# One core, gated cross attention and gated feed forward: the order of every engine's work laid out anew

## The chip, the core and the metric

The kernel runs on one core of one Trainium2 chip. The time is the device time of one execution in microseconds (us). A profile of another execution shows what every engine did. Engine names are those of the profile: PE is TensorE (its weight loads are PEld), DVE is VectorE, ACT is ScalarE, POOL is GpSimd, SP is SyncE, which here only issues transfers.

## The reference

Four batches of 512 rows with 256 columns. A layer norm, attention of 8 heads with depth 32 over a context whose mask in effect leaves the last 128 keys, a gated sum, another layer norm, and a feed forward of width 768 with integer weights.

```python
def attention(memory, query, mask, b):          # memory 4x512x512, query 4x512x256
    Q = split_heads(query, 8) * 32 ** -0.5
    K, V = (split_heads(part, 8) for part in jnp.split(memory, 2, axis=2))
    logits = jnp.einsum('bhqd,bhkd->bhqk', Q, K) + b[0] + -1e30 * (1 - mask)
    return merge_heads(softmax(logits) @ V)
def ffn(x, w_gate, w_up, w_down):               # weights int / 127
    h = silu(x @ w_gate.T) * (x @ w_up.T)
    return h @ w_down.T
x = x + tanh(g_xattn) * attention(ctx, layernorm(x), mask, b)
x = x + tanh(g_ffn) * ffn(layernorm(x), w_gate, w_up, w_down)
```

## The kernel before

The 2048 rows are worked in eight halves r = 0 to 7 of 256 rows; batch b has the halves 2b and 2b + 1. Values that must be exact go through TensorE as a high and a low float16 part. Every engine has its own instruction queue and works it strictly in order. The order is written out by hand: the table ORDER (L163) has one string of step codes per engine, and each engine's run() walks its string. A code is two letters, the half or batch, and after a dot a part. Semaphores alone hold the engines together: a step that needs another's result waits for a count.

The codes that the text uses, with the line of what they issue:

- sa (L968 to L977 on DVE, L658 on POOL): statistics of the first norm; na (L992 or L669) the norm, ha (L745) its high and la (L688) its low part. sa2, sa4 and sa6 take two halves at once. sb, nb, hb, lb are the same for the second norm (nb is L681).
- du (L1002, DVE): doubles the parts of q; qs (L1262) then turns them on TensorE for the halves 0 and 1, and qn (L591) turns them by two transfers on SP for the halves 2 to 7.
- kp, kr (L1048, L1040, L693): key parts; ks (L1272, L1277): key stack turned on TensorE and copied out by DVE (L1081, L1085) or ACT (L772). fr (L1013 to L1017) and ft (L1284, L1022) make the fillers that all key stacks but batch 0's need. br, mc, mt, eb are small steps for the mask. ys (L1059) is the scale of y.
- rm (L1333, and L1343 in batch 0, then L1122 on DVE): row maxima, four for each half; mx (L1358, L810) turns them. sc (L1378, L1380, then the exponential L821 on ACT): four for each half. ws (L1399, L1404, then L832, L834 on ACT): the weighing of the values. at (L1450 on PE, L1153 and L1155 on DVE, L698 on POOL): two for each half, adds the attention to x.
- nn (L582, SP): turns the second norm's parts by one transfer for the halves 0 to 6; nt (L1469, L860) does it on TensorE and ACT for half 7. wc (L781, ACT) casts a weight, wn (L573, SP) turns it; wn1 and wn0 are for hi, wn2 for do.
- hi (L1503): one of six hidden steps of a half, eight matmuls; ACT takes tanh (L869), pr (L1166, L1177) on DVE makes the product, hs (L878 on ACT, L705 on POOL) its two parts; do (L1529) is one of six down steps, four matmuls. fi (L939, L950, then L562, L559) adds and stores. ck, fs and sq check the ranges.
- wu (L1241): three or four matmuls on constants, whose results nobody reads. Ahead of all steps TensorE does 14 of them (L1218).

Work banks of PSUM are given out round robin by place in TensorE's string: four banks for the steps before hi0.0, and two from there on, since the other two belong to the hidden steps. A step that fills a bank waits until the one that used it last was emptied. hidden step n waits for product n - 2 (L1490). All loads are issued by SP and ACT ahead of their strings. The flag that is asked near the end decides whether a second, wide program follows; it does not here.

## Time and profile before

| | |
|---|---|
| time, median of 3 runs (range) | 137.76 us (137.49 to 138.76) |
| the profiled execution's own time | 137.66 us |
| its span, from the first to the last instruction | 135.8 us |
| PE busy | 125.0 us, 92% |
| DVE busy | 104.6 us, 77% |
| POOL busy | 94.0 us, 69% |
| ACT busy | 91.5 us, 67% |
| mean granted TensorE clock | 0.994 |

Busy time of PE counts a matmul from its start to its modelled end, so matmuls that follow each other overlap (an end stands 0.16 us behind the next start), and the distance between starts tells what one costs. A number in brackets at a row's end is the idle time ahead of it and what ended it.

### The profile page before, as it was taken

To read this page: it belongs to the slowest core of one execution; us is meant where nothing else is said; L and a number is where in the kernel's file an instruction comes from. 1 tells how busy PE (TensorE), PEld (TensorE's weight loads), DVE (VectorE), ACT (ScalarE), POOL (GpSimd) and SP (SyncE) were. 2 spreads that over 40 slices of the span, in tenths; PEclk is the share of its full clock that TensorE was granted. 3 is DMA by queue.
4 is the path that set the end of the run, shared out by engine and by line. 5 is a ranking of instruction groups with operands and counts; after the bars stand their busy time and mean duration, and the time that the engine had idled before them with its cause. 6 is when DMAs were issued, how large, how long until landed. Compare 5 with 4: busy or idle time off the path is not lost.

```text
span 135.8 us, 3716 instructions
## 1 busy us (share of the span) xinstructions
PE 125.0 (92%) x1276; PEld 97.6 (72%) x1276; DVE 104.6 (77%) x296; ACT 91.5 (67%) x206; POOL 94.0 (69%) x146
## 2 busy tenths in 40 slices
...
GB/s 127 285 127 369 370 352 155 119 186 89 83 157 116 77 5 76 97 58 7 0 165 234 69 2 57 25 0 0 75 84 0 5 233 1 77 7 47 30 86 92
DMA packets 32050, 14.08 MB, mean 104 GB/s; under 512 B 25605, under 2 KB 31257, under 8 KB 32025
## 3 DMA queue, kind: packets, MB, share of 16 engines
...
q14 instruction: 14, 0.11, 0.3%
...
HBM read 5.52 MB, written 2.10 MB: 56 GB/s over the span
## 4 chain that ended last, share of the span: by engine, by line
PE 60%; DVE 16%; POOL 9%; DMA 4%; issue 4%; SPq 3%; ACT 2%; DVEq 0%; ACTq 0%; POOLq 0%
PE ps L1503 26%; PE ps L1529 11%; DMA gates<-in_L_xattn_b_dram 4%; PE ps L1399 4%; PE ps L1404 4%; PE ps L1378 4%; PE ps L1380 4%; DVE max_cols L1122 4%; PE ps L1450 3%; PE ps L1333 2%; DVE stats L968 2%; POOL x_sb L698 2%; POOL h L705 2%; DVE gated L1166 2%; POOL q_parts L688 2%
## 5 line engine op out<-in xcount | busy, mean ns | idle before, releaser
L1503 PE MATMUL ps<-n_t,w_gu_t 128*128 128x256 f16 x384 | 49.0, 273 | 0.9 <-DVE h L1177 0.7
L1503 PEld LDWEIGHTS ps<-n_t,w_gu_t 128*128 128x128 f16 x384 | 36.4, 98 | 7.1 <-DVE h L1177 2.1
L705 POOL TENSOR_TENSOR h<-h 128x256 f16<-128x256 f32 x48 | 31.5, 674 | 7.5 <-ACT h L878 7.5
L1166 DVE SCALAR_TENSOR_TENSOR gated<-tanh_h,ps 128x256 f32<-128x256 f32 x48 | 19.9, 415 | 12.3 <-ACT tanh_h L869 11.9
L869 ACT ACTIVATE tanh_h<-ps 128x256 f32<-128x256 f32 x48 | 18.3, 382 | 13.1 <-PE ps L1503 10.9
L1529 PE MATMUL ps<-w_d_t,h 128*128 128x256 f16 x192 | 25.7, 273 | 0.0
L821 ACT ACTIVATE probs<-ps,exp_bias 128x512 f32<-128x512 f32 x32 | 21.6, 686 | 4.3 <-PE ps L1380 4.1
L1122 DVE TENSOR_REDUCE max_cols<-ps 128x4 f16<-128x512 f32 x32 | 21.4, 684 | 2.9 <-PE ps L1333 2.6
L1177 DVE SCALAR_TENSOR_TENSOR h<-ps,gated 128x256 f32<-128x256 f32 x48 | 20.4, 425 | 2.4 <-POOL h L705 0.8
L878 ACT ACTIVATE h<-h 128x256 f16<-128x256 f32 x48 | 18.5, 412 | 4.6 <-DVE h L1177 4.3
L1529 PEld LDWEIGHTS ps<-w_d_t,h 128*128 128x128 f16 x192 | 18.4, 98 | 2.1
L698 POOL TENSOR_TENSOR x_sb<-x_sb,attn 128x256 f32<-128x256 f32 x16 | 11.6, 733 | 8.7 <-DVE attn L1155 8.5
L1378 PE MATMUL ps<-q_stacks,k_stacks 128*128 128x256 f16 x64 | 15.6, 273 | 0.4 <-ACT max_rows L810 0.3
L1380 PE MATMUL ps<-max_rows,kv_rest 128*128 128x256 f16 x64 | 15.5, 273 | 0.0
L968 DVE BATCH_NORM_STATS2 stats<-x_sb 128x6 f32<-128x256 f32 x32 | 11.6, 413 | 4.6 <-DMA x_sb<-in_x_dram 2.5
L658 POOL TENSOR_TENSOR rstd<-var_eps,neg_half 128x2 f32<-128x2 f32 (+1 forms) x13 | 10.5, 806 | 6.7 <-DVE var_eps L977 6.6
L688 POOL TENSOR_TENSOR norm<-norm 128x512 f16<-128x512 f32 x8 | 9.3, 1160 | 6.4 <-ACT norm L745 6.2
L688 POOL TENSOR_TENSOR q_parts<-norm,q_parts 128x512 f16<-128x512 f32 x8 | 9.4, 1180 | 5.8 <-ACT q_parts L745 5.8
L1333 PE MATMUL ps<-k_stacks,q_stacks 128*128 128x128 f16 x128 | 12.1, 219 | 0.0
L1333 PEld LDWEIGHTS ps<-k_stacks,q_stacks 128*128 128x128 f16 x128 | 9.1, 98 | 2.3 <-issue 0.6
L681 POOL TENSOR_SCALAR norm<-x_sb,neg_mean,rstd 128x256 f32<-128x256 f32 x16 | 9.1, 579 | 0.5
L832 ACT ACTIVATE o_sb<-ps 128x512 f32<-128x512 f32 x8 | 4.8, 596 | 6.3 <-PE ps L1404 6.2
...
## 6 DMA issues: line engine op xcount, KB each, us to landing
...
q_stacks<-q_parts SPq DMA_TRANSPOSE x12, 3.3
```

Of the source, the lines that this page charges most:

```text
L688: pool.tensor_tensor(low, full, high, ALU.subtract).then_inc(norm_low, 1)
L705: pool.tensor_tensor(h16[:, r % 2, m, 1, :], h32[:, n % NHB, :], h16[:, r % 2, m, 0, :], ALU.subtract).then_inc(h_low, 1)
L821: act.activation(probs[:, j % NPB, :], bank32(SCORES[j % 2]), ACT.Exp, bias=key_bias[:, n:n + 1] if is_wide else exp_bias[:, b:b + 1], sca ...
L878: act.activation(h16[:, r % 2, m, 0, :], h32[:, n % NHB, :], ACT.Copy).then_inc(h_high, 1)
L1122: dve.tensor_reduce(dst, bank32(plan.bank(step)).rearrange("p (h k) -> p h k", h=HG), AX.X, ALU.max, negate=not is_wide).then_inc(emptied_ ...
L1166: mine(dve.scalar_tensor_tensor(out=gated[:, n % 2, :], in0=tanh_h[:, n % 2, :], scalar=1.0, in1=got[:, 0:SH], op0=ALU.add, op1=ALU.mult))
L1177: dve.scalar_tensor_tensor(out=dst, in0=got[:, SH:2 * SH], scalar=0.5 * W_SCALE * W_SCALE * H_SHRINK, in1=gated[:, n % 2, :], op0=ALU.mult ...
L1333: ins = pe.matmul(bank32(n)[:, j * P:(j + 1) * P], q_stacks[:, b, qt, h, :], k_stacks[:, b, h, :], start=(j == 0), stop=(b >= FILL_FROM an ...
L1378: pe.matmul(dst, k_stacks[:, b, h, :], q_stacks[:, b, 2 * half:2 * half + 2, h, :], start=(i == 0), stop=False, skip_group_check=True)
L1380: ins = pe.matmul(dst, (max_sel if is_wide else max_sel16)[:, h, :], (max_rows if is_wide else max_rows16)[:, rows, :], start=False, stop= ...
L1503: ins = pe.matmul(dst, lhs, rhs, start=(w == 0 and (k, l) == terms[0]), stop=(k, l) == terms[-1], skip_group_check=True)
L1529: ins = pe.matmul(dst, lhs, rhs, start=(m == 0 and l == 0 and (t == 0 or r == R - 1)), stop=(m == MT - 1), skip_group_check=True)
```

## The change: the five strings of the order

Only the strings of ORDER are other. Each engine has the same set of steps as before. The number of printed rows differs because equal neighbours are merged. The first line of PE's string, before and after, stands for the table:

```diff
     "pe": """
-        ks0 mt qs0.0 wu5 wu0 qs0.1 rm0.0 rm0.1 wu7 rm0.2 qs1.0 rm0.3 mx0 rm1.0 qs1.1 rm1.1 wu3 sc0.0 sc0.1 rm1.2 sc0.2
+        wu7 mt wu2 wu0 wu4 ks0 wu3 qs0.0 ft wu6 qs0.1 rm0.0 rm0.1 qs1.0 rm0.2 qs1.1 rm0.3 rm1.0 rm1.1 mx0 rm1.2 wu5
```

DVE at the program's start, from the first statistics of half 0 (`stats<-x_sb`). Before:

```order
L968 BN_STATS stats<-x_sb 128x6 x2
L972 BN_AGGR mv<-stats 128x2 x2
L977 TENSOR_REDUCE var_eps<-mv 128x2
L1048 TENSOR_SCALAR k_parts<-kv 128x8x64
L1007 TENSOR_SCALAR bias_row<-mask_row 1x128
L992 TENSOR_SCALAR norm<-x_sb,mv,rstd 128x256 x2
L1028 CAST mask_f<-mask_raw 16x128
L1040 TENSOR_TENSOR k_parts<-kv,k_parts 128x8x64
L968 BN_STATS stats<-x_sb 128x6 x2
L972 BN_AGGR mv<-stats 128x2 x2
L977 TENSOR_REDUCE var_eps<-mv 128x2
L1002 COPY q_parts<-q_parts 128x16x64
```

And the same place of DVE after the change:

```order
L968 BN_STATS stats<-x_sb 128x6 x2
L972 BN_AGGR mv<-stats 128x2 x2
L977 TENSOR_REDUCE var_eps<-mv 128x2
L1013 TENSOR_REDUCE neg_count<-mask_row 1x3
L1015 RECIPROCAL share<-neg_count 1x3
L1017 SCALAR_TENSOR_TENSOR fill_row<-mask_row,share 1x384
L992 TENSOR_SCALAR norm<-x_sb,mv,rstd 128x256 x2
L1048 TENSOR_SCALAR k_parts<-kv 128x8x64
L1028 CAST mask_f<-mask_raw 16x128
L968 BN_STATS stats<-x_sb 128x6 x2
L972 BN_AGGR mv<-stats 128x2 x2
L977 TENSOR_REDUCE var_eps<-mv 128x2
```

The fill row (three instructions) moved from behind four row maxima to a place ahead of the first norm, and the low part of the keys (L1040) behind the second statistics. The copy of the key stack (L1081), which before followed the first dup directly, now stands behind the paired statistics of halves 2 and 3.

TensorE at its start; `ones_b` are warm-ups, `k_parts` the key stack, `q_parts` a turned q. Before:

```order
L1218 MATMUL ps<-ones_b 128x512 x14
L1272 MATMUL ps<-ident,k_parts 128x128 x8
L1236 MATMUL ps<-ident,mask_f 128x16
L1262 MATMUL ps<-ident,q_parts 128x128 x8
L1241 MATMUL ps<-ones_b 128x512 x7
L1262 MATMUL ps<-ident,q_parts 128x128 x8
L1333 MATMUL ps<-k_stacks,q_stacks 128x128 x4
```

After:

```order
L1218 MATMUL ps<-ones_b 128x512 x14
L1241 MATMUL ps<-ones_b 128x512 x3
L1236 MATMUL ps<-ident,mask_f 128x16
L1241 MATMUL ps<-ones_b 128x512 x10
L1272 MATMUL ps<-ident,k_parts 128x128 x8
L1241 MATMUL ps<-ones_b 128x512 x3
L1262 MATMUL ps<-ident,q_parts 128x128 x8
L1284 MATMUL ps<-ident 128x384
L1286 MATMUL ps<-fill_row,ones 128x384
L1241 MATMUL ps<-ones_b 128x512 x3
L1262 MATMUL ps<-ident,q_parts 128x128 x8
L1333 MATMUL ps<-k_stacks,q_stacks 128x128 x4
```

Thirteen of the 25 warm-ups now stand ahead of the key stack and six more ahead of the first row max, and the fillers' matmuls (L1284, L1286) moved up from between the scores.

SP's queue behind the loads (`q_stacks` is a pair of qn, `w_gu_t` and `w_d_t` are weights, `n_t` is nn). Before:

```order
L591 DMA_TRANSPOSE q_stacks<-q_parts 128x8x128 x2
L573 DMA_TRANSPOSE w_gu_t<-w 128x12x128
L591 DMA_TRANSPOSE q_stacks<-q_parts 128x8x128 x2
L573 DMA_TRANSPOSE w_gu_t<-w 128x12x128
L582 DMA_TRANSPOSE n_t<-norm 128x8x128
L573 DMA_TRANSPOSE w_d_t<-w 128x12x128
L591 DMA_TRANSPOSE q_stacks<-q_parts 128x8x128 x2
L582 DMA_TRANSPOSE n_t<-norm 128x8x128
L591 DMA_TRANSPOSE q_stacks<-q_parts 128x8x128 x2
```

After:

```order
L591 DMA_TRANSPOSE q_stacks<-q_parts 128x8x128 x4
L573 DMA_TRANSPOSE w_gu_t<-w 128x12x128 x2
L591 DMA_TRANSPOSE q_stacks<-q_parts 128x8x128 x4
L582 DMA_TRANSPOSE n_t<-norm 128x8x128
L573 DMA_TRANSPOSE w_d_t<-w 128x12x128
L591 DMA_TRANSPOSE q_stacks<-q_parts 128x8x128 x2
L582 DMA_TRANSPOSE n_t<-norm 128x8x128
L591 DMA_TRANSPOSE q_stacks<-q_parts 128x8x128 x2
L582 DMA_TRANSPOSE n_t<-norm 128x8x128
```

The pairs of halves 4 and 5 moved ahead of the first n_t transpose, and the pair of half 7 ahead of the third.

Further on, TensorE's string has the row maxima rm4.0 to rm5.0, the key stacks of batch 2 and the first of batch 3, ws2, sc3.2 and mx4 ahead of hi0.0, which stood behind it; DVE has du5 and ys ahead of the products; and on ACT the first weight's cast stands ahead of the first exponentials, with the two others spread behind them.

## Rows read from the trace of the kernel before

**Rows 1.** Windows: us, busy us and instructions of each engine, clock, DMA share, GB/s
```profile
5.00:10.00 5.00, 2.73 (x25) 1.55 (x23) 4.33 (x18) 1.36 (x3) 2.91 (x3) 1.00 0.58 193
...
0.00:40.00 40.00, 34.06 (x330) 21.64 (x334) 32.82 (x105) 28.66 (x49) 29.15 (x53) 1.00 0.79 205
40.00:130.00 90.00, 89.13 (x939) 74.58 (x932) 70.59 (x189) 62.76 (x158) 64.20 (x93) 1.00 0.30 59
130.00:136.00 6.00, 1.81 (x17) 1.37 (x14) 1.18 (x3) 0.10 (x1) 0.67 (x1) 0.86 0.32 101
```

**Rows 2.** Timeline of PE, its waits: start us, us, instruction, count [idle before <-releaser]
```profile
0.97 4.95 PE L1218 MATMUL ps<-ones_b 128*128 128x512 bf16 x14 [0.97 <-POOL ones_b L629]
7.41 0.61 PE L1272 MATMUL ps<-ident,k_parts 128*128 128x128 f16 x8 [1.49 <-DVE k_parts L1040]
...
15.69 0.27 PE L1358 MATMUL ps<-ident,max_cols 128*128 128x128 f16 x2 [0.88 <-DVE max_cols L1122]
...
31.07 0.27 PE L1358 MATMUL ps<-ident,max_cols 128*128 128x128 f16 x2 [0.71 <-DVE max_cols L1122]
...
38.04 1.04 PE L1503 MATMUL ps<-n_t,w_gu_t 128*128 128x256 f16 x8
...
52.64 1.05 PE L1503 MATMUL ps<-n_t,w_gu_t 128*128 128x256 f16 x8 [0.73 <-DVE h L1177]
```

**Rows 3.** Timeline of PE, neighbours whose starts give the prices
```profile
26.61 0.61 PE L1333 MATMUL ps<-k_stacks,q_stacks 128*128 128x128 f16 x8
27.05 0.81 PE L1241 MATMUL ps<-ones_b 128*128 128x512 bf16 x3
27.70 0.39 PE L1333 MATMUL ps<-k_stacks,q_stacks 128*128 128x128 f16 x4
...
31.27 1.07 PE L1399 MATMUL ps<-probs,kv 128*32 128x256 f32 x16
...
33.14 0.40 PE L1333 MATMUL ps<-k_stacks,q_stacks 128*128 128x128 f16 x4
...
127.28 1.04 PE L1503 MATMUL ps<-n_t,w_gu_t 128*128 128x256 f16 x8
128.15 3.66 PE L1529 MATMUL ps<-w_d_t,h 128*128 128x256 f16 x32
```

**Rows 4.** Timeline of DVE, the front and the dup at 50 us
```profile
3.63 0.75 DVE L968 BATCH_NORM_STATS2 stats<-x_sb 128x6 f32<-128x256 f32 x2 [2.47 <-DMA x_sb<-in_x_dram]
...
12.47 0.68 DVE L1122 TENSOR_REDUCE max_cols<-ps 128x4 f16<-128x512 f32 x1
...
15.46 0.53 DVE L1013 TENSOR_REDUCE neg_count<-mask_row 1x3 f32<-1x384 int32 x1
...
17.56 0.67 DVE L1122 TENSOR_REDUCE max_cols<-ps 128x4 f16<-128x512 f32 x1
...
50.39 1.40 DVE L1002 COPY q_parts<-q_parts 128x1024 f16<-128x1024 f16 x1
```

**Rows 5.** Timeline of ACT, exponentials and a weight cast
```profile
18.42 1.27 ACT L821 ACTIVATE probs<-ps,exp_bias 128x512 f32<-128x512 f32 x2
...
21.23 1.50 ACT L781 ACTIVATE w<-w_raw 128x1536 f16<-128x1536 int32 x1
```

**Rows 6.** Timeline of SP's queue: start of the issue, us of issue
```profile
26.09 2.61 SPq L591 DMA_TRANSPOSE q_stacks<-q_parts  x2
...
34.70 1.23 SPq L582 DMA_TRANSPOSE n_t<-norm  x1
```

**Rows 7.** The page, parts 5 and 6: busy, mean ns | idle; us from issue to landing
```profile
L688 POOL TENSOR_TENSOR q_parts<-norm,q_parts 128x512 f16<-128x512 f32 x8 | 9.4, 1180 | 5.8 <-ACT q_parts L745 5.8
...
q_stacks<-q_parts SPq DMA_TRANSPOSE x12, 3.3
n_t<-norm SPq DMA_TRANSPOSE x7, 3.1
...
w_d_t<-w SPq DMA_TRANSPOSE x1, 5.8
```

**Rows 8.** Timeline of POOL, the last split of a product
```profile
130.17 0.67 POOL L705 TENSOR_TENSOR h<-h 128x256 f16<-128x256 f32 x1 [1.08 <-ACT h L878]
```

More of the change, by code:

```diff
@@ L164 @@
     "sp": """
-        qn2 wn1 qn3 wn0 nn0 wn2 qn4 nn1 qn5 nn2 nn3 qn6 fi0 qn7 nn4 nn5 fi1 nn6 fi2 fi3 fi4 fi5 fi6 fi7""",
+        qn2 qn3 wn1 wn0 qn4 qn5 nn0 wn2 qn6 nn1 qn7 nn2 fi0 nn3 nn4 fi1 fi2 nn5 nn6 fi3 fi4 fi5 fi6 fi7""",
     "pe": """
-        ks0 mt qs0.0 wu5 wu0 qs0.1 rm0.0 rm0.1 wu7 rm0.2 qs1.0 rm0.3 mx0 rm1.0 qs1.1 rm1.1 wu3 sc0.0 sc0.1 rm1.2 sc0.2
-        ft sc0.3 rm1.3 wu6 ws0 ks1.0 mx1 wu2 at0.0 ks1.1 at0.1 sc1.0 rm2.0 rm2.1 wu4 rm2.2 sc1.1 rm2.3 sc1.2 sc1.3
-        rm3.0 rm3.1 mx2 ws1 rm3.2 sc2.0 rm3.3 sc2.1 at1.0 sc2.2 at1.1 mx3 sc2.3 wu1 sc3.0 sc3.1 hi0.0 ws2 hi0.1 hi0.2
@@ L170 @@
-        at2.0 at2.1 sc3.2 hi0.3 ks2.0 hi0.4 rm4.0 ks2.1 hi0.5 do0.0 do0.1 sc3.3 rm4.1 do0.2 rm4.2 hi1.0 hi1.1 do0.3
-        rm4.3 hi1.2 ws3 hi1.3 mx4 hi1.4 at3.0 sc4.0 hi1.5 rm5.0 at3.1 sc4.1 do0.4 do0.5 ks3.0 sc4.2 hi2.0 sc4.3 rm5.1
-        hi2.1 ws4 hi2.2 rm5.2 hi2.3 at4.0 ks3.1 do1.0 hi2.4 rm5.3 at4.1 do1.1 do1.2 mx5 do1.3 hi2.5 rm6.0 hi3.0 do1.4
-        rm6.1 sc5.0 do1.5 hi3.1 sc5.1 hi3.2 sc5.2 rm7.0 hi3.3 sc5.3 rm6.2 hi3.4 ws5 rm6.3 do2.0 do2.1 at5.0 mx6 hi3.5
-        at5.1 do2.2 sc6.0 hi4.0 rm7.1 sc6.1 rm7.2 sc6.2 hi4.1 sc6.3 rm7.3 hi4.2 ws6 mx7 do2.3 hi4.3 do2.4 sc7.0 hi4.4
```

61 lines of the change are left out of this document (34 added, 27 removed).

## The prediction

> **What bounds the kernel now.** I read three views in this order. The windows come first: from 40 to 130 us TensorE is busy 89.13 of 90 us, before 40 us only 34.06 of 40, and the granted clock is 1.00, the 2.4 GHz level, in both [rows 1]. A busy TensorE in this profile is pipelined, so the timeline comes next, where I look at the distance from one start to the next. TensorE's opening warm-up ends at 5.92 us; after that it waits visibly before L1272 (1.49), L1358 (0.88 and 0.71) and once, far behind, before L1503 (0.73) [rows 2]. Third, the prices by distance of starts: eight 128-column matmuls take 0.44 us, three warm-up matmuls 0.65, one weigh step 1.87, one hidden step of eight 256-column matmuls 0.87 [rows 3]. So 0.055, 0.217, 1.86 and 0.109 per 256 columns. Summed over everything that TensorE does between 5.92 us and the start of its last step (384 hidden, 188 down and 128 score matmuls 76.4; 128 row-max matmuls and their eight bias matmuls 8.8; eight weigh steps 14.9; 48 float transposes 5.3; 25 warm-ups 5.4; the small rest 5.3) this is 116.1 us. The last step starts at 128.15 + 7 x 0.437 = 131.2 [rows 3], and 131.2 - 5.92 - 116.1 leaves 9.2 us in which TensorE started nothing. Of these, 6.9 lie ahead of the first hidden step at 38.04 [rows 2] (38.04 - 5.92 - 25.3 us of steps), 0.9 ahead of hi1.2 (0.73 [rows 2] and the 0.16 by which a matmul's end overlaps the next start), 0.3 ahead of hi6.3, and about 1.1 are a tenth behind each weigh step and the like.
>
> That is the frame: no step changes, so TensorE's 116.1 us stay, and the time moves by the change of those 9.2 us alone. What follows TensorE's last step (DVE, the store) is the same in both orders. All sums are made against the profiled execution, 137.66 us with a span of 135.8; the median of three is 137.76, 0.1 above it.
>
> **The front, walked.** I go through the new order with the durations of before; each step starts when its engine is free and its input is there.
> DVE. First statistics 3.63 to 4.78. Then comes the fill row, 2.10 us from its first to the row behind it (15.46 to 17.56) [rows 4], so the first norm begins at 6.9 and not at 5.81. Norm 0.65, key clamp 0.33, mask cast 0.13: 8.0. TensorE has done three warm-ups by 6.6 and waits 1.6 us for the cast; its next ten warm-ups end at 10.5. DVE does the second statistics (to 9.2), mask, bias row, dup of half 0, key rest (to 10.8), second norm, the paired statistics of halves 2 and 3 (2.0, to 13.4), and only then copies the key stack, to 14.0. The first row max can be multiplied from 14.1 (before 11.37) and DVE takes its maximum at 14.85, where before it was 12.47 [rows 4]. This is 2.4 us late. But what made it late is work that before stood behind it: fill row 2.1, dup 0.35, fillers 0.46 are done. DVE has no gap in either order from here to 30 us, and row max 1.3 (eighth maximum) ends at 22.7, where before it was 23.1.
> TensorE. max_t of half 0 at 18.0 (before 15.69 [rows 2]), first scores at 19.2 (17.78). ACT now casts the first weight, 1.5 us [rows 5], ahead of the four exponentials and not between them, so they run from 20.6 to 23.1 (0.6 each [rows 5]); TensorE waits 0.7 us for them and starts the first weigh step at 23.4 (21.56). Here the new order is 1.9 behind in place and 1.0 ahead in idle time: with 15.8 us of steps done at 25.3, 3.6 were lost (25.3 - 5.92 - 15.8) against 4.6 for almost the same steps of before.
> From there before loses 0.87 ahead of mx2, 0.42 ahead of sc2.0 and some 0.7 in three smaller waits, in a stage in which DVE's maxima arrive one at a time. In the new order rm2.3's maximum ends at 30.1, mx2 is at 30.15 (31.07 [rows 2]), the second weigh step at 30.45 (31.27 [rows 3]), and sc2.0 follows it at 32.5 without a wait, since TensorE has rm4, rm5 and the key stacks 2 and 3 ahead of hi0.0 to fill holes with. hi0.0 comes out at 39.95. That is later than 38.04, but 29.4 us of steps lie ahead of it and not 25.3 (rm4.0 to rm5.0 1.1, three key half stacks 0.65, ws2 1.86, sc3.2 0.44, mx4 0.11). Idle up to there: 39.95 - 5.92 - 29.4 = 4.6. **Term one: 6.9 - 4.6 = 2.3 us gained.**
>
> **The middle.** The wait at hi1.2 [rows 2] comes from DVE, which had a row max, the y scale and a dup of 1.40 us [rows 4] ahead of product 1.0. Dup 5 and y scale now stand far ahead. Walked on to mx5 at 57 us, products 0.0 to 1.1 are made 0.4 us or more before the hidden step two further on asks for them. **Term two: 0.9 gained.** The waits around 115 us stay (same chain, flag_sum between products 6.0 and 6.1).
>
> **The SP queue.** A q pair holds SP's queue for 2.61 us [rows 6], and what stands behind it waits. nn0 now stands behind qn4 and qn5. I find qn5 issued by 36.2 and POOL's low part of half 0 ready at 36.4 (its last step there is 1.18 long [rows 7]), so nn0, itself 1.23 us of issue [rows 6], leaves at 36.4 and lands 3.1 to 3.3 later [rows 7], at 39.6, against hi0.0 at 39.95: it costs nothing by 0.3 us. nn2 now stands behind qn7, leaves at 60.0 and lands at 63.1 to 63.3, against hi2.0 at 63.7. Bounds of such a landing: 3.1 below, 5.8 above, which the down weight's transpose took [rows 7]. I take 3.2, the n_t row itself, and charge 0.3 for both together. wn2 lands at 43.5 for a do0.0 at 47.6, also at 5.8.
>
> **The tail.** Before, 32 matmuls stand behind the last hidden step (from 128.15 [rows 3]); the POOL split of its product ends at 130.84 [rows 8], 2.7 us after that, and the last down step waits for it. Now hi7.3 and hi7.4 are back to back and six down steps, 2.6 us, lie in between and not seven: 0.1 plus 0.1 for hi7.5, which must wait for product 7.3. Bounds 0 and 0.5; I take 0.2.
>
> **Sum.** -2.3 - 0.9 + 0.3 + 0.2 = -2.7. The walk gave most hand-overs between engines nothing or 0.05 us, while a start behind another engine's end shows 0.03 to 0.1 in the rows. Some fifteen stand on the chain up to hi0.0, between 0 and 1.5 us; I take 0.7. That makes -2.0: span 133.8, time 135.7.
>
> **The clock.** TensorE keeps 1.00 in the slice from 5 to 10 us, where it is busy 2.73 of 5 us, and shows 0.86 from 130 us, where it stops [rows 1]. The new order has 3.4 us of work in the former slice, and its longest wait is 1.6 us against 1.49, so I charge nothing. The Trainium skill, TensorE: Matmul & The Clock Gate, section Part 4: PE-mode transpose, speaks against the change: it says that transposes do not hold the clock up as other matmuls do, and this order spends its warm-ups before a stretch with many transposes. By that rule the sum would be the one of rival 4; by the row it is unchanged.
>
> **Rivals.**
> 1. The front is not made up. If row max, mask and cast hand over later than walked and the weigh step's 1.9 us lag stays, ws1 comes at 33.2, hi0.0 at 42.6, and term one is -0.4 and not +2.3. Time 137.66 + 0.4 - 0.9 + 0.5 = 137.7: no change. For it: DVE's first maximum really is 2.4 late and ACT has a cast ahead of the exponentials. Against it: DVE, the engine without a gap there, gets the same work.
> 2. SP's queue decides. nn0 and nn2 have 0.3 and 0.5 us of slack. With landings of 5.8 they arrive at 42.2 and 65.8 and TensorE waits 2.3 and 2.1 us: -2.0 + 4.1 = +2.1, 139.8. It costs more than it saves from landings of 4.8 on. Against it: seven n_t transposes have a median of 3.1.
> 3. Half of either: one landing at 4.5, or 1 us of hand-overs more. 136.5 to 137.
> 4. A fall of the clock to 1.2 GHz between 13.4 and 18.6, where the new order has transposes and few warm-ups: 4.1 us of steps double, waits of 1.1 absorb a part, +3.0 - 2.0 gives 138.7. The rows of before show no such fall.
>
> **How the numbers follow.** Forecast (a gain of 1.4 to 3.4 us) 0.61; rival 1 0.11; rival 3 0.14; rival 2 0.10; rival 4 0.04. The time is 135.7. The range goes from 134.4 (the walk without hand-overs, 135.0, and without the 0.3 and 0.2) to 138.2, which holds rivals 1 and 3 and leaves out 2 and 4. About 1% is what a measurement of this kernel can tell from no change, that is 136.4 to 139.1. Faster: the forecast 0.61 and a little of rival 3, 0.63. Within 1%: rival 1, most of 3 and the mild end of 2 and 4, 0.26. Slower: 0.11.
>
> **What would show it.** Right: a first row-max maximum near 14.9 us, the first weigh step near 23.4 to 24, the second before 31.3, hi0.0 at 39.5 to 41, no wait of 0.5 us or more between 41 and 110, and a last matmul near 129.8. Wrong: a wait of L1503 on the n_t transpose at 40 or 64 us (rival 2), a first hidden step behind 42 us (rival 1), a slice below 1.00 before 25 us (rival 4). A DVE gap between 9 and 30 us would break the argument on which term one rests.

## The result and the profile after

| | before | after |
|---|---|---|
| time, median of 20 runs on one chip | 138.62 us (137.21 to 140.45) | 137.15 us (136.36 to 138.05) |
| ratio, 95% interval | | 0.9926, 0.990 to 0.995 |
| the profiled execution's own time | 137.66 us | 137.35 us |
| its span | 135.8 us | 135.5 us |

The changed kernel is 0.7% faster. The interval leaves out 1, so the gain is real, but it lies inside the 1% that the prediction took as no change. The ratio leaves out some executions of the kernel before that fell into a slower state, and is therefore nearer to 1 than the quotient of the two medians. Forecast was a gain of 2.0 us to 135.7 us; measured are 0.3 us between the two profiled executions and about 1.0 by the ratio.

The windows of the kernel after, in the columns of [rows 1]:

```profile
5.00:10.00 5.00, 4.35 (x23) 1.83 (x22) 4.83 (x21) 0.99 (x2) 2.28 (x3) 1.00 0.65 207
0.00:40.00 40.00, 36.38 (x366) 23.27 (x367) 34.31 (x107) 29.87 (x50) 30.84 (x55) 1.00 0.92 215
40.00:130.00 90.00, 87.80 (x902) 73.58 (x901) 67.69 (x189) 60.59 (x157) 61.33 (x90) 1.00 0.28 54
```

Before 40 us TensorE is busy 36.38 us where it was 34.06: the front works, and better than forecast. From 40 to 130 us it is busy 87.80 where it was 89.13. A stretch that was full in [rows 1] now has holes. The timeline of PE shows them; these are the starts of mx0 and mx2, for comparison with [rows 2], and its visible waits of over 0.5 us behind 20 us:

```profile
16.91 0.27 PE L1358 MATMUL ps<-ident,max_cols 128*128 128x128 f16 x2
...
28.88 0.27 PE L1358 MATMUL ps<-ident,max_cols 128*128 128x128 f16 x2 [0.29 <-DVE max_cols L1122]
...
34.92 0.38 PE L1333 MATMUL ps<-k_stacks,q_stacks 128*128 128x128 f16 x4 [1.19 <-DVE attn L1155]
...
41.39 0.39 PE L1503 MATMUL ps<-n_t,w_gu_t 128*128 128x256 f16 x2 [0.86 <-DMA n_t<-norm]
...
66.44 0.39 PE L1503 MATMUL ps<-n_t,w_gu_t 128*128 128x256 f16 x2 [1.14 <-DMA n_t<-norm]
```

The three are rm4.0, hi0.0 and hi2.0. With the 0.16 us by which a matmul's end overlaps the next start they are 1.34, 1.02 and 1.30 us, 3.66 together. None of them stands in [rows 2]. hi0.0 and hi2.0 name their cause, the n_t transposes nn0 and nn2. rm4.0 names DVE's attn, which had ended at 34.44. It multiplies q stacks, and the q transposes of half 4 were issued from 31.49 on, the first landing 3.34 later, at 34.83. So this too is a transpose on SP's queue, as x2 shows below. The queue in the kernel after:

```profile
31.49 5.44 SPq L591 DMA_TRANSPOSE q_stacks<-q_parts  x4
37.04 1.35 SPq L582 DMA_TRANSPOSE n_t<-norm  x1
...
58.96 2.73 SPq L591 DMA_TRANSPOSE q_stacks<-q_parts  x2
61.80 1.70 SPq L582 DMA_TRANSPOSE n_t<-norm  x1
```

TensorE's idle time, counted from the end of the opening warm-up (5.92 before, 6.02 after) to the start of do7.5 (131.21 and 130.89), less its 116.1 us of steps (the rows not shown are further ones of the same timelines; the prediction has 6.9 for the first figure, its subtraction gives 6.82):

```
                                              before   after
idle ahead of the step named in the last line    6.82    3.12
hi1.2 (product 1.0)                              0.89    0
rm4.0 and rm4.2                                  -       1.62
hi0.0 on nn0                                     0       1.02
hi2.0 on nn2                                     0       1.30
the rest, to do7.5                               1.47    1.71
sum                                              9.18    8.77
first line counted up to                         hi0.0   mx3
```

Between mx3 and hi0.0 the kernel after has no idle time but that at rm4.0, rm4.2 and hi0.0, so the first line holds all idle time up to hi0.0 that is not a wait for SP's transposes. It fell by 3.7 us, and the middle gained 0.9. Then 3.94 were given back, all at transposes that SP issues.

### The profile page after: what moved, and what is told of

Its sections match the earlier page's. It is cut to its first block, busy times and chain, and to the rows that moved or that the text cites. A ratio compares the mean times of both kernels' runs of the same rounds, so it can differ in the third digit from the quotient of the medians.

```text
span 135.5 us, 3716 instructions
## 1 busy us (share of the span) xinstructions
PE 125.6 (93%) x1276; PEld 97.7 (72%) x1276; DVE 103.1 (76%) x296; ACT 90.5 (67%) x206; POOL 92.8 (68%) x146
## 4 chain that ended last, share of the span: by engine, by line
PE 57%; DVE 21%; DMA 9%; SPq 6%; issue 5%; DVEq 0%; ACT 0%
PE ps L1503 28%; PE ps L1529 13%; DMA n_t<-norm 7%; DVE max_cols L1122 6%; SPq L591 6%; DVE stats L968 5%; PE ps L1399 3%; PE ps L1450 3%; PE ps L1404 3%; PE ps L1380 2%; PE ps L1378 2%; DMA x_sb<-in_x_dram 2%; DVE q_parts L1002 2%; PE ps L1333 1%; DVE mv L972 1%
## 5 line engine op out<-in xcount | busy, mean ns | idle before, releaser
L1503 PE MATMUL ps<-n_t,w_gu_t 128*128 128x256 f16 x384 | 49.0, 273 | 2.2 <-DMA n_t<-norm 2.0
L1503 PEld LDWEIGHTS ps<-n_t,w_gu_t 128*128 128x128 f16 x384 | 36.5, 98 | 8.7 <-DMA n_t<-norm 2.4
L1529 PE MATMUL ps<-w_d_t,h 128*128 128x256 f16 x192 | 26.5, 273 | 0.1
L688 POOL TENSOR_TENSOR q_parts<-norm,q_parts 128x512 f16<-128x512 f32 x8 | 9.3, 1161 | 5.9 <-ACT q_parts L745 5.9
L688 POOL TENSOR_TENSOR norm<-norm 128x512 f16<-128x512 f32 x8 | 9.3, 1161 | 4.0 <-ACT norm L745 3.9
L1399 PE MATMUL ps<-probs,kv 128*32 128x256 f32 x128 | 8.6, 385 | 0.0
```

What stands on the lines that cost most here:

```text
L688: pool.tensor_tensor(low, full, high, ALU.subtract).then_inc(norm_low, 1)
L1503: ins = pe.matmul(dst, lhs, rhs, start=(w == 0 and (k, l) == terms[0]), stop=(k, l) == terms[-1], skip_group_check=True)
L1529: ins = pe.matmul(dst, lhs, rhs, start=(m == 0 and l == 0 and (t == 0 or r == R - 1)), stop=(m == MT - 1), skip_group_check=True)
```

## Why the front gained more

DVE, from the first statistics on, in the kernel after (L1013 to L1017 are the fill row, L992 the first norm):

```profile
3.41 0.75 DVE L968 BATCH_NORM_STATS2 stats<-x_sb 128x6 f32<-128x256 f32 x2 [2.26 <-DMA x_sb<-in_x_dram]
...
4.58 0.54 DVE L1013 TENSOR_REDUCE neg_count<-mask_row 1x3 f32<-1x384 int32 x1
5.15 0.16 DVE L1015 RECIPROCAL share<-neg_count 1x3 f32<-1x3 f32 x1
5.35 0.55 DVE L1017 SCALAR_TENSOR_TENSOR fill_row<-mask_row,share 1x384 f16<-1x384 int32 x1
5.82 0.72 DVE L992 TENSOR_SCALAR norm<-x_sb,mv,rstd 128x256 f32<-128x256 f32 x2
...
13.68 0.69 DVE L1122 TENSOR_REDUCE max_cols<-ps 128x4 f16<-128x512 f32 x1
```

The walk priced the fill row at its 2.10 us of [rows 4] and put the first norm at 6.9. It is 1.24 us here and the norm starts at 5.82. The dear part in before was L1017 alone, 1.41 us beside the making of a low part on POOL (L688), against 0.55 here:

```profile
15.46 0.53 DVE L1013 TENSOR_REDUCE neg_count<-mask_row 1x3 f32<-1x384 int32 x1
16.02 0.17 DVE L1015 RECIPROCAL share<-neg_count 1x3 f32<-1x3 f32 x1
16.22 1.41 DVE L1017 SCALAR_TENSOR_TENSOR fill_row<-mask_row,share 1x384 f16<-1x384 int32 x1
```

```profile
16.06 1.16 POOL L688 TENSOR_TENSOR q_parts<-norm,q_parts 128x512 f16<-128x512 f32 x1 [0.74 <-ACT q_parts L745]
```

L688 had started first and ended at 17.22; L1017 ended 0.41 behind it. The same distance, 0.40 to 0.41 us, stands in the three other traces in which L1017 starts inside an L688 (x4, x7 and x11, where it took 1.38, 1.23 and 1.23). In the kernel after POOL makes only its rstd beside it, up to 5.45. The first row maximum came at 13.68, 1.2 before the forecast 14.85, and the weigh steps at 22.23 and 29.08 (forecast 23.4 and 30.45; before 21.56 and 31.27). The Trainium skill, SBUF — State Buffer, section SBUF: two separate sides, says that DVE and GpSimd share a port pair and that a DVE instruction with two SBUF inputs is blocked by a GpSimd instruction that reads SBUF and started first. L1017 reads mask_row and share. The traces agree: 1.41 and 0.55 us for the same instruction, and the fixed distance behind L688's end.

## Experiments on the three waits

Each ratio below is to the kernel before, run on the same chip.

**x1: nn2 ahead of qn7.** `nn1 qn7 nn2 fi0` becomes `nn1 nn2 qn7 fi0` in SP's string; nothing else.

> The changed kernel with one swap in SP's string: nn2 stands ahead of qn7 and not behind it. In the profile of the changed kernel hi2.0 waits 1.30 us (start 66.44, end of the step before 65.14) for the n_t transpose, which is issued at 61.80 behind the pair qn7 (58.96) and lands 4.6 us later. Theory F (instruction fetch): a 16 KB packet of the instruction queue at 61.9 us stops every transpose in flight for about 1.7 us; nn2, now issued at 60.95, is in flight then and still needs 4.6 to 5.0 us, landing 65.6 to 65.9, so hi2.0 still waits 0.4 to 0.8 us and the gain is 0.5 to 0.9 us of 137.2. Theory Q (queue place alone): the place behind the pair made it late; issued at 60.95 it lands 3.1 to 3.3 us later at 64.2, the wait is gone and the gain is 1.3 us. Either: rm7.0 may wait for qn7 if that lands behind 67.6.

136.02 us, ratio 0.9843 (0.979 to 0.990). hi2.0 starts at 64.80 without a wait; the other two waits are 0.94 and 1.17 here. nn2 landed in 4.0 us, between the two expectations.

**x2: wn0 first.** `qn2 qn3 wn1 wn0 qn4` becomes `wn0 qn2 qn3 wn1 qn4`.

> The changed kernel with wn0 moved to the head of SP's string, where SP is idle from 13.3 to 20.9 us and the weight's cast is done at 19.5. Theory that three late transposes ate the front's gain: qn4 is then issued at about 30 us (when du4 is done) and not at 31.49, lands at 33.3, rm4.0 does not wait (1.34 us before), nn0 leaves at 35.6 and not 37.04, and hi0.0 waits 0.3 us or less (1.02 before): a gain of 1.8 to 2.4 us against the changed kernel, about 135. Rival: the waits only stand in for another limit (DVE's maxima, ACT's exponentials); then the same TensorE steps wait for those engines, and the gain is 0 to 0.5 us.

136.33 us, ratio 0.9855 (0.980 to 0.991). rm4.0 starts at 34.19 without a visible wait. In the kernel after, in x1 and here it starts 0.09 to 0.10 us behind the landing of the first q transpose of half 4 (34.83, 34.51 and 34.09), so that is what it had waited for, whatever the row named. hi0.0 (1.09) and hi2.0 (1.30) still wait. The expectation had 0.3 or less at hi0.0 and a time of about 135: nn0 left at 36.18 and not at 35.6, and took 4.39.

**x5: both.**

> The kernel after, with two entries of SP's order moved: the transpose of wn0 first of all, and nn2's ahead of qn7's. Each alone gave 0.9855 and 0.9843 of the kernel before. Theory F (a fetch of TensorE's instructions holds up the transposes in flight, and a transpose behind a held one starts later still): the waits ahead of rm4.0 (1.34) and hi2.0 (1.30) both go, the one ahead of hi0.0 (about 1.0) stays, since a fetch at 37 to 39 us still falls on nn0. TensorE's idle time falls by 2.4 us against the kernel after, less what the idle time further on gives back; each alone brought only 1.1 of its 1.3, so I expect 134.9 to 135.4 us, ratio 0.975 to 0.979 to before. Theory Q (only the place in SP's queue counts): the same two waits go and hi0.0's stays, same time; this run doesn't tell the two apart but gives the price of the waits together. Rival G: the gains of the two don't add, because the end is held by something later (DVE's products behind 105 us): then 136.0, ratio 0.984.

135.07 us, ratio 0.979 (0.974 to 0.985): as forecast, and the gains add within the intervals. Waits of PE from 24 to 68 us, in the kernel after and then in x5 (total, times, longest):

```profile
PE ps L1503 <- DMA n_t<-norm: 2.0, 2, 1.1
PE ps L1333 <- DVE attn L1155: 1.2, 1, 1.2
PE ps L1358 <- DVE max_cols L1122: 0.3, 1, 0.3
```

```profile
PE ps L1503 <- DMA n_t<-norm: 0.8, 1, 0.8
PE ps L1358 <- DVE max_cols L1122: 0.3, 1, 0.3
```

## Why the landings are long

A wait comes of a late issue, a long landing, or both. The landings of nn0 and nn2 were 4.3 and 4.6 us, those of n_t in [rows 7] 3.1. While each was in flight, the packet records show a packet of 16,384 bytes on a queue of another kind, q8, starting at 38.5 and at 61.9 us. Part 3 of the page of the kernel after counts them:

```profile
## 3 DMA queue, kind: packets, MB, share of 16 engines
q1 hardware_dynamic: 31984, 13.77, 46.3%
q8 instruction: 12, 0.20, 0.6%
```

The packets are 0.9 to 1.5 us long and, but for the last, 7 to 17 us apart. From some 0.4 us behind the start of the one at 61.9, for about 1.2 us, the transposes' 256-byte packets all but stop:

```
packets of SP's queue per 0.5 us, from    61.0 61.5 62.0 62.5 63.0 63.5
after (q8 packet starts at 61.9)           345  354  167    7   19  379
x3    (q8 packet starts at 56.1)           420  390  336  340  102  502
```

If q8 carries TensorE's instructions, its times depend on how many TensorE issues, and not on SP's order.

**x3: other instruction counts.** The 39 warm-up matmuls of 512 columns become 78 of 256: same columns, same order on every engine.

```
-            for _ in range(FIRST_WARM_UP):
-                pe.matmul(bank32(Y_BANK), ...to_broadcast((P, HG, P)), ...)
+            for _ in range(2 * FIRST_WARM_UP):
+                pe.matmul(bank32(Y_BANK)[:, 0:2 * P], ...to_broadcast((P, 2, P)), ...)
```

> The changed kernel with each of the 39 warm-up matmuls of 512 columns replaced by two of 256: the same columns and the same TensorE time, but 78 more instructions (matmuls and weight loads) ahead of the rest, so each fetch of 256 instructions comes about 3.4 us earlier: 24.3, 35.1, 45.4 and 58.5 us, not 27.7, 38.5, 48.8 and 61.9. Theory F: the pair qn7, issued at 58.96, and nn2 behind it land after 3.1 to 3.4 us and not 5.0, 5.2 and 4.6; hi2.0's wait falls from 1.30 to 0.2 us or less. The transposes qn2 and qn3 that are in flight at 24.3 take 5 us in their place, and rm2.2 waits for them up to 1 us. In total -1.5 to +0.5 us. Theory Q: the landings stay as they were (5.0 to 5.2 at 59 to 60 us) and so does the wait of 1.30.

136.16 us, ratio 0.9845 (0.980 to 0.990). It does the same work as the kernel after in more instructions, and is 0.8% faster. The q8 packet comes at 56.1 rather than 61.9 (58.5 was expected), and hi2.0's wait is gone. As expected another wait came: the first q pair, issued at 20.98 with a packet at 23.5, took 4.76 and 4.27, and rm2.0 waits 1.20. rm4.0's wait is gone behind it, and hi0.0's is 0.48.

**x15: cut into four.** A further 78 instructions.

> The kernel after, its warm-ups cut into 156 of 128 columns. With whole ones qn7, qn7, nn2 take 5.00, 5.24, 4.60 us (fetch at 61.9), with 78 halves 3.21, 3.96, 3.45 (fetch at 56.1). Theory F: if the fetch here lies outside 59 to 66 us the three take under 4.0 again and hi2.0 doesn't wait; if it lies inside, at least one takes over 4.4. Theory Q: 5.0, 5.2, 4.6 as with whole ones, hi2.0 waits 1.3, time 137.0 to 137.3.

137.80 us, ratio 0.990 (0.986 to 0.994). The packet is back at 62.4 (one more has passed ahead of it) and so is the wait, 1.22. Here both theories had forecast a wait; x3 and x15 together tell them apart. The SP queue's rows of the kernel after, x3 and x15 for the last q pair and nn2 (duration of the issue in ns, min/median/max; then issue to landing in us):

```profile
L591 SPq DMA_TRANSPOSE q_stacks<-q_parts x2: 1232/1342/1452, 59.0 to 60.2; - x2
...
DMA to landing us min/median/max: 5.0/5.1/5.2
```

```profile
L591 SPq DMA_TRANSPOSE q_stacks<-q_parts x2: 1232/1284/1336, 58.3 to 59.6; - x2
...
DMA to landing us min/median/max: 3.2/3.6/4.0
```

```profile
L591 SPq DMA_TRANSPOSE q_stacks<-q_parts x2: 1232/1354/1477, 59.5 to 60.7; - x2
...
DMA to landing us min/median/max: 4.9/5.0/5.2
```

Of all runs that keep the order qn7, qn7, nn2:

```
         q8 packet   first issue   landings (us from issue)
after      61.9        58.96        5.00  5.24  4.60
x2         61.2        58.19        5.00  5.24  4.61
x7         66.3        63.25        5.03  5.27  4.63
x8         62.2        59.26        5.00  5.24  4.62
x15        62.4        59.46        4.89  5.16  4.50
x3         56.1        58.32        3.21  3.96  3.45
x11        58.5        60.49        3.18  3.95  3.44
```

Against x3 and x11, a packet some 3 us behind the first issue costs 1.8, 1.3 and 1.2 us. The same holds for nn0: 3.0 to 3.2 us where no such packet starts within 3 us behind its issue (before, x9, x10), and 3.7 to 5.0 where one does (the kernel after and the thirteen others). In before nn0 was issued at 34.70 and landed before the packet at 39.7. The n_t transposes that stand alone (no other transpose issued in the 4.5 us ahead and the 3.1 us behind) leave the place in the queue out of it. In the 17 traces 66 of them have no packet starting within 3 us behind their issue and land in 3.03 to 3.10 us; 14 have one and take 3.44 to 4.74. There is no exception. The Trainium skill, Runtime: NRT & Kernel Launch, section Instruction fetch mechanics, says that an engine's instructions are fetched in blocks of 16 KiB over a DMA queue of its own and that this is mostly hidden. Size and dependence on TensorE's count agree with the traces. Whether TensorE itself ever waits for a fetch was not looked at; a transpose in flight pays 0.3 to 1.8 us.

The queue has a share of its own. With nn2 first (x1, x5, x6, x9, x12 to x14) it takes 4.0 us and the two behind 3.2 to 3.6, wherever the packet lies ahead of it (56.1 to 64.2). That is the 4.0 of x1 which neither theory had. Why the first of the three then takes 4.0 was not tried.

**x4: the kernel before, cut as in x3.**

> The same splitting of the warm-ups in the kernel before, the other way round: there the fetches of 32.0 and 39.7 us fall beside the transposes that matter (nn0 is issued at 34.70 and lands at 37.95, hi0.0 starts at 38.04). 3.4 us earlier they fall at 28.6 and 36.3. Theory F: nn0 lands after about 5 us, at 39.6, hi0.0 waits 1.2 to 1.7 us, and the kernel is 1.0 to 1.7 us slower than before. Theory Q: no transpose changes, no wait at hi0.0, the time within 0.3 us of before.

140.58 us, ratio 1.014 (1.008 to 1.020). In its profile a q8 packet at 38.8 lies upon nn0 (issued 35.86, landing 5.00) and hi0.0 waits 1.69 us, which the profiled execution of the kernel before did not. But that execution took 141.90 us and shows a granted clock of 0.91 from 5 to 10 and 0.75 from 10 to 15 us, so how the 1.9 us divide is open.

**x13 and x14: x5, cut in two and in four.**

> The kernel with wn0 first and nn2 ahead of qn7 (135.07 us; fetches at 27.8, 37.6, 47.9, 58.1 us; hi0.0 waits 1.01 for nn0, issued 35.86, landing 4.50), with the 39 warm-up matmuls of 512 columns cut into 78 of 256: the same columns, the same order. Theory F (fetches): the fetches come 1 to 5 us earlier each, landings change where a fetch leaves or enters; those of nn0 at 3.9 to 4.3, so hi0.0's wait is 0.3 to 0.8 rather than 1.01, and some transpose that took under 3.6 us takes over 4.2 in the new place (likely the pairs issued at 21 to 24 us, with a wait of up to 1.2 ahead of rm2.0). Time 134.6 to 135.2, ratio 0.974 to 0.980. Theory Q (place in the queue): every landing within 0.2 us of the kernel with whole warm-ups, hi0.0's wait 0.9 to 1.1, time 135.0 to 135.2.

> The same with the warm-ups cut into 156 of 128 columns (117 instructions more). Theory F: the fetches move by up to 10 us against the uncut kernel, one more of them falls ahead of 60 us, and landings over 4.2 us are those whose flight a fetch overlaps, whichever they are: I can't say beforehand which, but none over 4.2 without a fetch between issue and landing among the q and n transposes of the first 70 us, save nn1's. Time between 134.3 (no wait on a landing) and 136.6 (a wait of 1.3 ahead of hi0.0 and of one other). Theory Q: landings within 0.2 us of the uncut kernel's, time 135.0 to 135.2.

x13: 137.08 us, ratio 0.985 (0.980 to 0.989). The packet at 24.4 falls on the first q pair (5.23, 4.40, 4.04), rm2.0 waits 1.89, and nn0, later by that, meets the packet at 38.0 and takes 4.52: hi0.0 still waits 1.01. I had expected that wait to shrink and 134.6 to 135.2 us: a miss, though the wait ahead of rm2.0 was the one feared. x14: 135.69 us, ratio 0.976 (0.972 to 0.980): waits of 0.75 and 1.27, on a chip on which the kernel before took 139.07. Its interval and that of x5 overlap. The same program is thus worth 0.976 to 0.985 by nothing but how its warm-ups are cut.

## Experiments on the last wait

In x5 only hi0.0 waits, 1.01 us. nn0 leaves at 35.86, right behind POOL's low part (35.77).

**x6: x5 with nn0 ahead of qn5, POOL's lb0 ahead of kp3, TensorE's ks3.0 and rm5.0 later.**

> The kernel after with all three waits on transposes taken on: SP's order wn0 qn2 qn3 wn1 qn4 nn0 qn5 wn2 qn6 nn1 nn2 qn7 (nn0 ahead of qn5), POOL makes the low part of half 0 ahead of key part 3 (lb0, kp3), TensorE runs key stack 3.0 behind sc3.0, and row max 5.0 stands behind hi0.0, sc3.3 on TensorE and behind product 0.0 and at2.0 on DVE. Theory F and the queue together: nn0 is issued before 35.5 and lands before 40.0 even with a fetch upon it (4.6 us), so hi0.0 starts by 40.2 without a wait over 0.3, rm4.0 and hi2.0 neither; TensorE's idle time is 3.3 us less than after's: 133.9 to 134.6 us, ratio 0.967 to 0.973. Rival G (a bound of DVE or ACT behind the waits): hi0.0 comes early, but waits of over 0.5 us appear behind it at products or scores, and the time stays above 135.0.

136.26 us, ratio 0.989 (0.982 to 0.996). hi0.0's wait is gone, but ks3.0 waits 1.17, up to 37.20. Both things that it needs came at one time: kp3, which POOL now ended at 36.95, and its bank, which DVE's row maximum emptied at 36.96. Which of the two held it was not separated; the text of x9 below names kp3 alone. rm6.0 waits 0.55. Another wait took over, as rival G has it.

**x9: the whole chain earlier.** As x6, but with ks3.0 behind ws2, and also sb0 ahead of du4 on DVE, lb0 ahead of la5 on POOL, hb0 one exponential earlier on ACT.

> The faster kernel with wn0 first and nn2 ahead of qn7 (135.07 us), in which only the wait of 1.0 us ahead of hi0.0 is left. There nn0 was issued at 35.86, right behind POOL's low part of half 0 (35.77), and landed 4.5 later. Here that part is made earlier: the second statistics of half 0 ahead of dup 4 on DVE, the low part ahead of q part 5 and key part 3 on POOL, its cast behind the first exponential of half 2 on ACT; nn0 goes ahead of qn5 in SP's queue; the steps that need q part 5 and key part 3 (row max 5.0, key stack 3.0) stand later on TensorE. Theory (the wait ahead of hi0.0 is POOL's chain plus a landing that a fetch of instructions lengthens): nn0 is issued at 34.0 to 34.8 and lands by 39.3 even at 4.6 us, hi0.0 starts at 39.4 to 39.8 with no wait of 0.3 or more, and the whole takes 133.9 to 134.6 us, ratio 0.968 to 0.974. Rival G (another engine takes the wait over, as POOL's key part 3 did ahead of key stack 3.0 in the kernel without the three waits, where it cost 1.17): a wait of 0.5 to 1.2 us on key stack 3.0, row max 5.0 or row max 6.0, and the time stays between 134.9 and 135.8.

141.42 us, ratio 1.028 (1.023 to 1.034). nn0 left at 35.19 and landed in 3.04, but mx3 waited 5.01. PE's row names max_cols on DVE. One step further back, on DVE:

```profile
31.35 0.68 DVE L1122 TENSOR_REDUCE max_cols<-ps 128x4 f16<-128x512 f32 x1
36.24 1.36 DVE L1002 COPY q_parts<-q_parts 128x1024 f16<-128x1024 f16 x1 [4.21 <-POOL q_parts L688]
```

du5 needed the la5 that I had moved behind lb0 on POOL, and two row maxima stood behind du5. Neither the forecast nor its rival had this.

**x12: du5, rm5 and rm6 moved behind that.**

> The kernel with the low part of half 0 made early (141.42 us) with its fault mended: there DVE's dup 5 stood ahead of row max 3.2 and needs q part 5, which had been put behind the low part on POOL (done 36.21), so DVE stood 4.2 us and TensorE 5.0 us ahead of mx3. Here dup 5 stands behind row max 4.1, row maxes 5.0, 5.1 and 6.0 behind hidden steps 0.2 and 0.3 on TensorE and behind the first two products on DVE. Theory (hi0.0 waits for POOL's chain and a landing that a fetch lengthens): mx3 at 33.0 to 34.0 without a wait, nn0 issued at 34.9 to 35.3, landed by 39.8 at 4.6 us or 38.4 at 3.1; hi0.0 at 39.2 to 39.9 with a wait under 0.4, and the whole 134.0 to 134.8 us, ratio 0.970 to 0.977 to before, against 0.979 for the kernel with only wn0 and nn2 moved. Rival G (another engine takes the wait over): hi0.0 earlier than 40.0, but waits of 0.5 to 1.2 on row max 5.0 or 6.0 or mx5, and the time between 134.9 and 136.0.

137.21 us, ratio 0.996 (0.993 to 0.999), where 134.0 to 134.8 had been expected. nn0 left at 34.90 and landed at 38.59, 3.69 later with a packet at 37.4; in x9, without one, it had taken 3.04. hi0.0 has no wait, but the step ahead of it has one: mx4 waits 1.02 us, since du6 on DVE waits 1.15 for la6 on POOL and rm4.3 stands behind it.

```profile
39.07 0.94 DVE L1002 COPY q_parts<-q_parts 128x1024 f16<-128x1024 f16 x1 [1.15 <-POOL q_parts L688]
39.93 0.68 DVE L1122 TENSOR_REDUCE max_cols<-ps 128x4 f16<-128x512 f32 x1
```

Three times the last microsecond moved to another wait. POOL has no gap of over 0.2 us from 18.4 to 38.2 us in x5, so what is pulled forward there pushes something else back.

## Experiments on the front and the clock

**x7: the fill row late.** In the kernel after, fr back behind rm0.3, its use ft behind rm1.2 (DVE) and sc0.1 (TensorE).

> The kernel after, but the fill row (fr, 1.24 us of DVE there) is put back where the kernel before has it, behind row max 0.3, and its use (ft) back behind row max 1.2 on DVE and score 0.1 on TensorE. Theory E (in the kernel after the fill row fills the time in which DVE waits for the first half's rstd, and it runs while POOL's share of DVE's memory port is free): the first norm still starts at 5.8 us, since it waits for rstd and not for DVE; the first row maximum stays at 13.7 or comes a little earlier; all maxima from 1.0 on come 1.2 to 2.1 later, ws0 comes at 23 to 24 rather than 22.2, and the time is 0.8 to 1.6 us above that of the kernel after, ratio to before 0.999 to 1.006. Rival W (the prediction's walk: DVE has no gap, so it is the same wherever it stands): the first norm starts at 4.8 to 5.0 and the first maximum at 12.4 to 12.6, ws0 within 0.3 of 22.2, and the time within 0.4 us of after's, ratio 0.990 to 0.995.

140.69 us, ratio 1.019 (1.013 to 1.025). Early, the fill row filled a hole in DVE, as theory E has it; here the hole is bare:

```profile
5.66 0.74 DVE L992 TENSOR_SCALAR norm<-x_sb,mv,rstd 128x256 f32<-128x256 f32 x2 [0.84 <-POOL rstd L658]
```

The first norm starts at 5.66, the first maximum is taken at 13.62. But the loss against the kernel after is 3.5 us and not 0.8 to 1.6. TensorE waits long for the fillers, and the granted clock falls (columns of [rows 1]; the profile is of its slowest execution, 141.89 us with a mean clock of 0.968, the others have 0.972 to 0.988):

```profile
23.33 0.58 PE L1277 MATMUL ps<-fillers,k_parts 128*128 128x128 f16 x4 [2.86 <-DVE fillers L1022]
```

```profile
20.00:25.00 5.00, 2.14 (x16) 1.44 (x15) 4.93 (x17) 0.78 (x3) 3.07 (x5) 0.69 0.23 50
25.00:30.00 5.00, 5.00 (x45) 2.44 (x44) 2.56 (x12) 3.53 (x5) 1.98 (x3) 0.62 0.89 170
```

**x11: the same, with 14 warm-up matmuls (3.0 us) in that hole (wu1, moved there and grown from 3).**

> The kernel with the fill row late (140.69 us), in which TensorE stood 3.0 us ahead of key stack 1.0 and the granted clock fell below 1.00 from 21 to 31 us. Here 14 of the warm-up matmuls (3.0 us) run in that hole instead of none. Theory: the 3.5 us that it lost against the kernel after are two things, DVE's fill row (some 2.3 us in place, of which the front gives 1 to 1.5 to the end) and a fall of the clock (the rest). With the hole filled the clock stays at 1.00 (above 0.97 in each slice of the front), mx1 comes where it did or up to 1.0 earlier, and the time is 138.0 to 139.3, ratio 0.997 to 1.006. Rival: the clock's fall costs nothing since DVE bounds that stretch: time as it was, 140.2 to 141, ratio 1.014 to 1.020. Rival 2: filling doesn't hold the clock (it falls for another reason, the core's whole load): slices below 0.95 as before.

137.95 us, ratio 1.001 (0.998 to 1.004).

```profile
20.00:25.00 5.00, 4.80 (x36) 2.71 (x33) 4.93 (x17) 1.39 (x3) 3.08 (x5) 1.00 0.32 72
25.00:30.00 5.00, 4.52 (x64) 3.61 (x65) 4.74 (x16) 5.00 (x10) 3.54 (x5) 1.00 0.99 189
```

The clock stays at 1.00, and 1.9% of the time come back, 2.6 us. Not all of that is the clock's: hi2.0 waits 1.32 in x7 and not at all here, since the packet came at 58.5, ahead of qn7. That leaves about 1.3 us for the fall of the clock by the ratios. Up to hi0.0 the two profiled executions differ by 2.8 (45.68 and 42.92), but x7's is 1.2 above its median. Against the kernel after 0.8% is left, about 1.1 us, again with hi2.0's wait gone. The first weigh step is 3.2 us later than there (25.48). So the fill row's place is worth about 1 us with that wait gone and would be worth more with it.

**x8: no warm-ups behind the opening ones but wu7.** 22 matmuls, 4.8 us of TensorE, left out.

> The kernel after with 22 of its 25 warm-up matmuls behind the opening ones left out (wu0 to wu6; wu7 stays). They take 4.8 us of TensorE. Theory D (up to the second weigh step TensorE waits for DVE and ACT, so what it does in between costs nothing, and the clock stays at 1.00 without them): mx0 stays at 16.9 within 0.2 us, ws0 at 22.2 within 0.3, the granted clock 1.00 in every slice up to 130 us, and the time within 0.5 us of after's, ratio 0.988 to 0.995; the fetches of TensorE's instructions move later, by the 22 records, and with them the waits ahead of hi0.0 and hi2.0 may change by up to 1 us. Rival C (the warm-ups hold the clock, rival 4 of the prediction): the granted clock falls below 0.95 in one or more slices from 5 to 30 us, the transposes and row-max matmuls there take up to twice as long, and the time is 1 to 3 us above after's, ratio 1.000 to 1.015. Rival T (TensorE bound in the front, so that less work gains): ws0 at 21.5 or before and 1 us or more gained.

137.81 us, ratio 0.998 (0.994 to 1.002), 0.6% above the kernel after. ws0 at 22.31 and ws1 at 29.21, within 0.15 us of it: up to there TensorE waits for DVE and the warm-ups cost nothing. In the profiled execution the clock does fall, to 0.66 from 10 to 15 us, behind a wait of 2.04 us:

```profile
9.76 0.83 PE L1272 MATMUL ps<-ident,k_parts 128*128 128x128 f16 x8 [2.04 <-DVE k_parts L1040]
```

```profile
10.00:15.00 5.00, 4.95 (x50) 4.02 (x48) 4.73 (x18) 3.51 (x7) 3.55 (x5) 0.66 1.10 365
```

The steps there were slower and still in time for DVE. It doesn't fall each time: five executions have a mean clock of 0.987 like the profiled one, six have 0.994 to 1.000, and their medians are 137.97 and 137.63 us. So the fall costs some 0.3 us of the 0.8; what the rest is, is not shown.

**x10: in the kernel before, the fill row early and nothing else.**

> The kernel before with one piece of the change alone: the fill row stands behind the first statistics on DVE (and the first norm ahead of key part 0 and bias row), as in the kernel after, and no longer between row max 0.3 and 1.0. In before DVE has 0.49 us of idle time ahead of the first norm and the fill row takes 2.10 us beside POOL's norm; early it took 1.24. Theory E: the first norm begins 0.0 to 0.2 later than 5.81, the first maximum 0.3 to 0.8 later than 12.47, row max 1.0 1.2 to 1.8 earlier than 17.56, the first weigh step up to 0.8 earlier, and TensorE's idle time up to mx3 shrinks by 0.6 to 1.4 us: 136.9 to 137.9 us, ratio 0.990 to 0.996. Rival W (the prediction's walk: only moved, no gain): everything up to row max 0.3 2.1 us later, row max 1.0 where it was, time within 0.4 us of before, ratio 0.998 to 1.003.

138.33 us, ratio 1.0015 (0.998 to 1.006): no gain, though the row did shrink to 1.25 us and the norm stayed at 5.72. The profile shows why half-way: the first maximum came at 13.72 (12.47 before), and DVE then stood 0.94 and 0.92 us ahead of rm0.0 and rm1.0, while TensorE ran at a clock of 0.77 from 10 to 15 us. But the clock is not why nothing was gained: the six executions with a mean clock of 0.993 or more took 137.21 to 138.62 us, median 137.95, against 137.76 for the kernel before. So the early fill row brings nothing by itself. That it needs the rest of the order is argued and not shown.

## Why the prediction was wrong

The frame held: TensorE's 116.1 us of steps stayed and the time moved with its idle time.

- **Term one** was 2.3 and came out at 3.7 (6.82 to 3.12), counted as the prediction did, without SP's transposes. The walk had the first norm 1.1 too late, at 6.9 and not 5.82, and everything behind it too: it priced the fill row at 2.10 where it took 1.24, and the first statistics ended 0.2 earlier. The first two weigh steps were 1.2 and 1.4 ahead of the walk.
- **Term two**, 0.9, came out as forecast; hi1.2 doesn't wait.
- **The SP queue** is the step that failed. It was charged 0.3 and cost 3.94 us (1.34 + 0.28 at rm4.0 and rm4.2, 1.02, 1.30). Four things were wrong in it. The landing of 3.2 was taken from the median of [rows 7]; in the new order both transposes had a fetch upon them, 4.3 and 4.6. They also left later than walked, nn0 at 37.04 and not 36.4, nn2 at 61.80 and not 60.0. The forecast gave them slack against the walked hi0.0 of 39.95; without SP's waits hi0.0 would have been at 38.75 (an estimate: 41.39 less 1.02 and 1.62), and that takes the slack away, so what is gained ahead of a fixed landing is not a gain. And the q transposes of half 4, behind wn1 and wn0, were not walked at all, though they are in the same queue.
- **The tail**: hi7.4 and do7.5 wait 0.24 and 0.22, 0.46 together, where 0.2 was charged with bounds of 0 and 0.5.
- **Hand-overs**, 0.7: the front came earlier than the walk that had none, so nothing of this charge shows. Whether they cost something that the cheap fill row covered was not separated.
- **The clock** stayed at 1.00 in every slice up to 130 us, rival 4 did not come; the longest wait behind the opening warm-up is 1.34. It does come in other orders of this kernel: with waits of 2.04 (x8), 3.0 (x7) and 5.01 us (x9, 0.88 from 40 to 50 us). But it came with shorter ones too. In x4 the rows of L1272 and L1262 show waits of 0.85 and 0.77 and in x10 of 1.43 and 0.62, and the clock was 0.91 and 0.89 from 5 to 10 us, 0.75 and 0.77 from 10 to 15; the kernel before has 1.49 and 0.78 there and kept 1.00. So no run here gives the wait that brings the fall, and that none was charged came out right without a rule behind it. The Trainium skill, TensorE: Matmul & The Clock Gate, section Part 4: PE-mode transpose, says that transposes do not engage the full clock. In x8 it fell in a stretch of transposes, in x7 in one of other matmuls around a wait, and the kernel after kept 1.00 through the same transposes with warm-ups among them. The traces decide neither for the transposes nor against them.
- **Rivals.** Rival 2 (SP's queue decides) is what happened, and its sign, a wait of L1503 on the n_t transpose at 40 or 64 us, came at 41.39 and 66.44. It cost 3.6 us beyond what was charged, nearly the 4.1 it was priced at. Its landings of 5.8 and its condition, landings of 4.8 on, were not met: 4.3 and 4.6, nearer to rival 3's 4.5, were enough, since the transposes left late and a third one waited too. It came on top of a front 2.1 us better than the forecast with its 0.7 for hand-overs and so ended at 137.15 and not at 139.8. It had 10%. The range was to leave rival 2 out, and it held the time only because two errors, 2.1 too little in the front and 3.6 too little in the queue, offset each other: luck. The evidence for more stood in [rows 7]: a landing of 5.8 asked for a cause, and I called it a bound. That transpose was issued at 35.98, and a q8 packet starts at 39.7.

The sum with the measured terms: -3.70 - 0.89 + 3.94 + 0.24 for the rest, the tail's 0.46 among it, = -0.41 us of idle time. The opening warm-up ended 0.1 later and what follows do7.5's start took 0.1 longer; that gives the 0.2 to 0.3 between the two spans. The ratio says 1.0; the kernel before spreads over 3 us on that chip, its profiled execution of 137.66 us is faster than the median of 138.62, and of that difference no profile here tells more.
